# Paired values, maxima in a free row, fp16 triples for K, Q and V, and a loop written out, in a Swin block on one Trainium2 core

## The reference

```
y = roll(ln(x, norm1_g, norm1_b), (-3, -3));  yw = windows(y)            # (B*64, 49, 128)
q, k, v = heads(yw @ qkv_w.T + qkv_b)                                    # 16 heads of 8
attn = softmax(q * 8**-0.5 @ k.T + bias(rel_pos_table) + shift_mask)
o = windows_back((attn @ v) @ proj_w.T + proj_b);  x = x + roll(o, (3, 3))
h = gelu(ln(x, norm2_g, norm2_b) @ fc1_w.T + fc1_b) @ fc2_w.T + fc2_b
return x + h
```

## Time and profile before

| | us |
|---|---|
| median of 3 runs | 4402.23 (4398.28 to 4403.39) |
| the profiled execution | 4409.18, span 4407.4 |
| PE busy | 4134.3 (94%) |
| ACT busy | 2889.0 (66%) |
| DVE busy | 2743.0 (62%) |
| POOL busy | 2014.4 (46%) |
| DMA | 443.34 MB, mean 101 GB/s, q1 32.4% of 16 engines |
| mean granted TensorE clock | 0.983 of full speed |

### The profile page before, as it was taken

The page is one execution under the profiler, slowest core; times in us unless marked ns, Lnnn a source line. Parts: engine busy times, 40 slices in busy tenths (PEclk is TensorE's granted clock), DMA queues, the critical chain, the costliest instruction groups (busy, mean ns, idle before and its releaser), DMA issues.

```text
span 4407.4 us, 179808 instructions
## 1 busy us (share of the span) xinstructions
PE 4134.3 (94%) x72586; PEld 3265.2 (74%) x72586; DVE 2743.0 (62%) x6930; ACT 2889.0 (66%) x5120; POOL 2014.4 (46%) x3472
## 2 busy tenths in 40 slices
PE   3999999999999999999999999999999999999998
PEld 2777777777777777777777777777777777777777
DVE  5666665666656656566565656666566566666663
ACT  2666666666666666666666666766666666666665
POOL 4444444444444444444444444444444444444443
PEclk8999999999999999999999999999999999999999
DMA  2333333333333333333333333333333333333332
GB/s 77 102 106 102 98 105 97 105 102 98 105 99 104 109 95 101 98 105 102 99 104 97 105 101 99 105 101 102 94 105 105 99 104 107 104 104 105 106 106 62
DMA packets 626000, 443.34 MB, mean 101 GB/s; under 512 B 158451, under 2 KB 624611, under 8 KB 625059
## 3 DMA queue, kind: packets, MB, share of 16 engines
q1 hardware_dynamic: 624595, 428.82, 32.4%
q0 software_dynamic: 464, 1.81, 0.1%
HBM read 106.07 MB, written 51.46 MB: 36 GB/s over the span
## 4 chain that ended last, share of the span: by engine, by line
PE 82%; ACT 9%; issue 4%; DVE 3%; SPq 1%; DMA 0%; POOL 0%; ACTq 0%; POOLq 0%; DVEq 0%
PE ps L782 18%; PE ps L752 11%; PE ps L766 10%; PE ps L704 10%; PE ps L816 8%; PE ps L739 7%; PE ps L734 7%; PE ps L850 5%; PE ps L796 3%; DVE neg_max L576 2%; ACT L411 2%; ACT v_own L491 2%; PE ps L809 2%; ACT hid L435 2%; ACT probs L418 2%
## 5 line engine op out<-in xcount | busy, mean ns | idle before, releaser
L576 DVE TENSOR_REDUCE neg_max<-ps 113x16 f32<-113x784 f32 x1024 | 998.1, 975 | 514.5 <-PE ps L704 489.4
L418 ACT ACTIVATE probs<-ps 113x784 f32<-113x784 f32 x1024 | 841.1, 822 | 476.1 <-PE ps L739 470.5
L782 PEld LDWEIGHTS ps<-w,hid 128*112 128x112 f32 x7168 | 845.2, 181 | 49.7 <-issue 18.9
L782 PE MATMUL ps<-w,hid 128*112 128x128 f32 x7168 | 865.9, 277 | 0.0
L435 ACT ACTIVATE hid<-ps,col 128x448 f32<-128x448 f32 (+1 forms) x1024 | 541.6, 585 | 420.9 <-PE ps L766 417.8
L739 PE MATMUL ps<-st_q,st_k 128*49 128x196 f16 x8192 | 701.3, 250 | 4.2 <-issue 4.2
L734 PE MATMUL ps<-bias,eye_k 108*64 108x392 f16 x4096 | 686.6, 332 | 0.0
L752 PE MATMUL ps<-probs,v_own 113*32 113x49 f32 x32768 | 584.8, 211 | 101.0 <-issue 71.2
L752 PEld LDWEIGHTS ps<-probs,v_own 113*32 113x32 f32 x32768 | 438.4, 110 | 275.9 <-issue 245.7
L704 PE MATMUL ps<-mx_k,mx_q 128*49 128x196 f16 x8192 | 547.3, 254 | 20.6 <-DMA mx_k<-k_hi 9.3
L739 PEld LDWEIGHTS ps<-st_q,st_k 128*49 128x49 f16 x8192 | 447.0, 105 | 129.2 <-issue 7.1
(11 more groups left out here) (81 smaller groups left out, 6471.9 us busy)
## 6 DMA issues: line engine op xcount, KB each, us to landing
st_k<-k_hi SPq DMA_DIRECT2D x256, 196.0 KB
st_q<-q_hi SPq DMA_DIRECT2D x1024, 49.0 KB
oT_raw<-pv_sb SPq DMA_DIRECT2D x256, 196.0 KB, 2.6
x_in<-in_x SPq DMA_DIRECT2D x224, 196.0 KB
x_res<-in_x SPq DMA_DIRECT2D x224, 196.0 KB
out_y<-y_out SPq DMA_DIRECT2D x224, 196.0 KB
mx_q<-q_hi SPq DMA_DIRECT2D x128, 196.0 KB
mx_k<-k_hi SPq DMA_DIRECT2D x512, 49.0 KB
```

The source lines that it names most:

```text
L418: nc.scalar.activation(probs[0:KP, w % 2, :].rearrange("p (b c) -> p b c", b=2), ps[0:KP, b:b + 2, 0:HB * WT], ACT.Exp).then_inc(s_exp, 1)
L576: nc.vector.tensor_reduce(neg_max[0:KP, :, w, :], ps[0:KP, 0:2, 0:HB * WT].rearrange("p b (h k) -> p b h k", k=WT), AX_X, ALU.max, negate= ...
L782: last = mm(tokens_of(6)[0:TP, i, :], hid[:, c, i * TP:(i + 1) * TP], w_2[:, c, :], start=(c == 0), stop=(c == CH - 1))
```

## The change

- The hardware loop is gone: `turns` writes all 133 turns out, and every semaphore wait has a constant. The extra semaphore increments of `apart` are gone too.
- The norm's scale and shift (norm1) go into the weights and biases at set-up. ACT writes `yT` as a plain copy (now in the memory of `oT`). DVE splits it into fp16 `yT_hi` and `yT_lo` (new, L599 and L601). K, Q and V each become three fp16 matmuls where there was one in fp32; V takes both images of a window in one stationary operand of 128 columns.
- The negated maxima go by DMA to row 32e + 3 of `st_q`, whose partner rows in `st_k` are set to 1. So `bias` no longer depends on the window, and keeps one copy. The layouts of q, k, `neg_max` and the maxima's PSUM follow.
- Values are multiplied for two pairs of windows (u) at once; `probs` has four buffers; the copy out of PSUM takes both.
- The order of each body changes: on PE the first part of fc2 comes ahead of the transposes, K and Q come after the second part of fc2, all of fc1 comes before V, and each second logits are cut in two. On DVE the reciprocal comes first, and the second copy of V after `x1`. On ACT all gelus come before V's copies.

The diff, cut to its core:

```diff
-        def turns(eng, body):
-            def plain(a, b):
-                for t in range(a, b):
-                    body(t, lambda n: n >= EDGE, lambda k: (t + k) % 2)
-            plain(-2, LOOP_1[0])
-            with eng.Fori(LOOP_1[0], LOOP_1[1] - UNROLL + 1, UNROLL) as t:
-                for later in range(UNROLL):
-                    body(t + later, lambda n: False, lambda k: (LOOP_1[0] + later + k) % 2)
-            plain(LOOP_1[1], STEPS + 3)
+        def turns(body):
+            for t in range(-2, STEPS + 3):
+                body(t, lambda n: n >= EDGE, lambda k: (t + k) % 2)
...
@@ SP: the maxima
-                    for par in range(2):
-                        for im in range(2):
-                            row = MAX_ROWS + im
-                            sp.dma_start(bias[row:row + 1, par, :, :].rearrange("p w c -> p (w c)"),
-                                         neg_maxT[HP * par:HP * (par + 1), im, :]).then_inc(s_neg_dma, 16)
+                    for e in range(EQ):
+                        row = 32 * e + MAX_ROW
+                        sp.dma_start(st_q[odd(0)][row:row + 1, e, :, :].rearrange("p g c -> p (g c)"),
+                                     neg_maxT[32 * e:32 * (e + 1), :, :]).then_inc(s_neg_dma, 16)
...
@@ ACT
-                        return nc.scalar.activation(o, a, ACT.Identity, scale=col[:, G1:G1 + 1],
-                                                    bias=col[:, B1:B1 + 1])
+                        return nc.scalar.activation(o, a, ACT.Copy)
...
@@ DVE: new, ahead of h_lo and behind the reciprocal
+                    high, low = (y[odd(1)][:, :, :, 0:WT].rearrange("p w m q -> p m w q") for y in (yT_hi, yT_lo))
+                    flat = yT[:, :, :, :]
+                    nc.vector.tensor_copy(high, flat).then_inc(s_y_hi, 1)
+                    dve.wait_ge(s_y_hi, n + 1)
+                    nc.vector.tensor_tensor(low, flat, high, ALU.subtract).then_inc(s_y_lo, 1)
...
@@ PE: K and Q
-                    pe.wait_ge(s_yT, n + 1)
-                    for wt, bank in ((w_k, 0), (w_q, 4)):
-                        for im in range(2):
-                            mm(ps[:, bank + im, 0:BT], wt[:, :], yT[odd(1)][:, im, :, :].rearrange("p w q -> p (w q)"),
-                               start=True, stop=True).then_inc(s_qk, 1)
+                    pe.wait_ge(s_y_hi, n + 1)
+                    high, low = ([y[odd(1)][:, :, im, 0:WT] for im in range(2)] for y in (yT_hi, yT_lo))
+                    for w_hi, w_lo, bank in ((wk_hi, wk_lo, 0), (wq_hi, wq_lo, 4)):
+                        for im in range(2):
+                            mm(ps[:, bank + im, 0:BT], w_hi[:, :], high[im], start=True, stop=False)
+                            mm(ps[:, bank + im, 0:BT], w_lo[:, :], high[im], start=False, stop=False)
+                        if bank == 0:
+                            pe.wait_ge(s_y_lo, n + 1)
+                        for im in range(2):
+                            mm(ps[:, bank + im, 0:BT], w_hi[:, :], low[im], start=False, stop=True).then_inc(s_qk, 1)
...
@@ PE: V
-                            for im in range(2):
-                                last = mm(ps[HP * im:HP * im + WT, 6 + b, (w % 4) * C:(w % 4 + 1) * C],
-                                          yT[odd(0)][:, im, w, :], w_v[:, :], start=True, stop=True)
+                            for part, (yy, ww) in enumerate(((yT_hi, wv_hi), (yT_lo, wv_hi), (yT_hi, wv_lo))):
+                                last = mm(ps[:, 6 + b, (w % 4) * C:(w % 4 + 1) * C],
+                                          yy[odd(0)][:, w, :, :].rearrange("p m q -> p (m q)"), ww[:, :],
+                                          start=(part == 0), stop=(part == 2))
...
@@ PE: the attention loop
-                for w in range(NW):
-                    if exists(t):
-                        logits(t, w, edge, odd(0))
-                    if exists(t) and w > 0:
-                        pv(t, w - 1)
-                    if exists(t + 1):
-                        max_logits(t + 1, w, edge)
+                for u in range(NU):
+                    if exists(t):
+                        logits(t, 2 * u, edge, odd(0), (0, 1))
+                        logits(t, 2 * u + 1, edge, odd(0), (0,))
+                    if exists(t + 1):
+                        max_logits(t + 1, 2 * u, edge)
+                    if exists(t):
+                        logits(t, 2 * u + 1, edge, odd(0), (1,))
+                        if u > 0:
+                            pv(t, u - 1)
+                    if exists(t + 1):
+                        max_logits(t + 1, 2 * u + 1, edge)
```

More of the change, by code:

```diff
@@ L43 @@
 BT = NW * WT
+NU = NW // 2
 TP = 2 * W
@@ L182, in exists @@
         def exists(n):
-            return not isinstance(n, int) or 0 <= n < STEPS
+            return 0 <= n < STEPS
         def past(n, k):
-            return not isinstance(n, int) or n > k
+            return n > k
         def loads(n, edge):
@@ L265, in body @@
                 n = t + 2
-                if exists(n) and not (isinstance(n, int) and n == 0):
+                if exists(n) and n != 0:
                     sp.wait_ge(s_t1, n)
@@ L396, in body @@
                     norm(n, s_ln2, mv2, ve2, s_ve2, rs2, s_rs2, mr2, s_mr2, nm2, s_nm2, x1, z2, s_t2, s_z2)
-            turns(pool, body)
+            turns(body)
         @block.scalar
@@ L480, in body @@
                     load_table(ACT.Gelu)
-                    for m in range(6):
+                    for m in range(2 * CH):
                         gelu(t - 2, m)
+                if exists(t):
+                    load_table(ACT.Exp)
                 n = t
@@ L491, in body @@
                         nc.scalar.activation(v_place(1, b), v_made(1, b), ACT.Copy).then_inc(s_vown_b, 1)
[L492 to L494 removed]
                 if exists(t):
[L496 removed]
                     for w in range(NW):
                         exp_pair(t, w)
[L499 to L502 removed]
+                        if w % 2 and w > 1:
+                            copy_pv(t, w // 2 - 1)
+            turns(body)
         @block.vector
@@ L566, in finish @@
                     if past(n, 0):
-                        dve.wait_ge(s_stored, loads(n - 1, edge(n) and (not isinstance(n, int) or edge(n - 1))))
+                        dve.wait_ge(s_stored, loads(n - 1, edge(n) and edge(n - 1)))
                 dve.wait_ge(s_fc2, 2 * n + p + 1)
@@ L668, in body @@
                             aggregate(n, st2, s_st2, mv2, s_ln2)
-            turns(dve, body)
+            turns(body)
         @block.tensor
@@ L680, in _, with group @@
                    start=True, stop=True)
+            pe.wait_ge(s_inita, 2)
+            for c, ww in enumerate((w_q, w_k, w_vp)):
+                last = mm(ps[:, 7, 3 * C + c:3 * C + c + 1], ww, col[:, B1:B1 + 1], start=True, stop=True)
+            last.then_inc(s_w_split, 1)
             pe.wait_ge(s_bv, 1)
-            mm(ps[0:TP, 7, 0:C], bv_wide[:, :], w_p[:, :], start=True, stop=True).then_inc(s_bp_mm, 1)
+            mm(ps[0:TP, 6, 0:C], bv_wide[:, :], w_p[:, :], start=True, stop=True).then_inc(s_bp_mm, 1)
             pe.wait_ge(s_inita, 2)
             pe.wait_ge(s_init, 2)
-            def group(im, bank, g):
-                return ps[HP * im:HP * im + WT, bank + g // 2, (g % 2) * EQ * WT:(g % 2 + 1) * EQ * WT].rearrange(
-                    "p (e q) -> p e q", e=EQ)
+            def group(im, bank, g, step):
+                first = (g % 2) * step
+                return ps[HP * im:HP * im + WT, bank + g // 2, first:first + EQ * WT].rearrange("p (e q) -> p e q", e=EQ)
             def max_logits(n, w, edge):
@@ L730, in logits @@
                 kind = 2 * edge(n) + (w == NW - 1)
                 bank = 2 + 2 * (w % 2)
-                for b in range(2):
+                for b in banks:
                     for im in range(2):
                         mm(ps[HP * im:HP * (im + 1), bank + b, 0:HB * WT], eye_k[0:BIAS_ROWS, kind, im, :],
-                           bias[0:BIAS_ROWS, b, w, :], start=True, stop=False)
+                           bias[0:BIAS_ROWS, b, :], start=True, stop=False)
                     for g in (2 * b, 2 * b + 1):
@@ new lines, in pv @@
+            def pv(n, u):
+                pe.wait_ge(s_exp, NW * n + 2 * u + 2)
+                if u < 2:
+                    pe.wait_ge(s_vown, 2 * n + u + 1)
+                    pe.wait_ge(s_vown_b, 2 * n + u + 1)
+                else:
+                    pe.wait_ge(s_pv_sb, NU * n + u - 1)
+                for w in (2 * u, 2 * u + 1):
+                    for h in range(NH):
+                        g, r = h // NR, h % NR
+                        first = (2 * g + w % 2) * WT
+                        last = mm(ps[32 * r:32 * r + VC, 6 + u % 2, first:first + WT],
+                                  v_own[0:KP, w, h, :], probs[0:KP, w % 4, h * WT:(h + 1) * WT], start=True, stop=True)
@@ L837, in body @@
                 if exists(t - 2):
-                    fc1(t - 2, 4)
```

(3 more changed lines are left out.)

251 lines of the change are left out of this document (125 added, 126 removed).

## The result

The changed kernel takes **4233.77 us** (4232.79 to 4236.54, 4 runs) against 4402.81 for the kernel before in the same session: ratio 0.9619, 95% interval [0.9602, 0.9635]. The direction was forecast, the size was not: −169 us where −34 stood. Its profiled execution took 4236.54 us, span 4234.7.

The account below looks back on a forecast made before the run. It took PE, busy 4134 of 4407 us, plus its losses between matmuls as the bound. From the profiled 4409.2, −144 written out, +105 for turns of 33.28 us, +5 set-up gave 4375, so 4368 us at the median; range 4270 to 4450.

Parts of the forecast that it names:

- part 1: Loop written out: 103 intervals fall to 32.45 us each, −144 us, of which 82 are the 12 returns.
- part 3: End of a turn: PV and first fc2 quarter before L796's transposes remove PE's wait for the last maxima, −0.76 us.
- part 5: Maxima behind the projection: PE waits 1.0 us more before the second maxima matmuls, then 0.1 more three times a turn.
- part 2: Matmuls: fp16 K and Q save 0.67 us a turn, V 0.48; PV of two windows and the maxima's free row nothing.
- part 4: Front of the turn: waits for y_high and y_low add 0.83 us around K, late q_low 0.6 before fc1's later groups.
- set-up: PSUM clear, ten small steps on the weights and four POOL clears before the turns: 0 to 10 us, taken as +5.
- inner losses: Small losses inside a pass of the loop, 0.68 us in each of 91 intervals, 62 us, taken as gone.
- Rival B: Straight code loses in fetching what the loop body lost: 4430 us, or 4455 if all turns lose it; chance 0.14.
- The argument from 20 turns without losses: The last 20 turns, straight code behind the loop, take 32.45 us without the small losses, so written-out turns should too.
- Rival C: V's fp16 matmuls gain nothing and PE does 0.48 us more a turn, 61 us: 4429 us; chance 0.08.
- Rival A: y_high and y_low come in time, so 0.83 and 0.6 us a turn fall away, 183 us: 4185 us; chance 0.08.
- Rival D: The softmax sums land at the late bound, y_high 1.5 us later, +190 us: 4560 us; chance 0.05.

Follow-up runs that it names:

- run 1: The kernel before with its loop written out and nothing else changed, its own matmuls and order kept: 4288.68 us, ratio 0.9734 to the kernel before.
- Run 7: The changed kernel with first maxima matmuls ahead of all second logits and DVE's second copy of V moved to ACT: 4219.07 us.
- run 3: The changed kernel with the values of a pair split again, one window before the logits and one behind: 4317.08 us.
- run 4: The changed kernel with DVE's reciprocal moved behind the cast and the subtraction: 4184.31 us.
- run 11: The changed kernel with reciprocal behind the split, maxima matmuls ahead of logits, V's second copy on ACT, and probabilities and copied V in fp16: 4022.47 us.
- run 2: The changed kernel with K, Q and V back in fp32, without DVE's cast and subtraction: 4294.64 us.

## Why the prediction was wrong

The three runs that undo one part each give the change in its parts, beside what the forecast's own steps gave them:

| part | forecast | measured |
|---|---|---|
| written out (part 1) | −144 | −116 |
| order, pairs, free row (part 3, part 5, the PV of part 2): (−0.76 + 1.0 + 0.3) x 128 | +69 | +6 |
| triples (part 2, 4): (−0.67 − 0.48 + 0.83 + 0.6) x 128 | +36 | −61 |
| set-up | +5 | within the others |
| sum | −34 | −171 |

The measured parts run from the 4404.75 of the kernel before in the session of run 1; they come from three sessions, so each is good to some 5 us. By the prediction's own mark, half a us from 33.3, it is wrong: the mean turn is 32.20.

**Part 1 was right in kind and 28 us too large.** The returns are gone: no interval near 39. The 62 us of inner losses were taken as gone, and they are the step that failed: 22 of them stay in run 1. They had also been counted too wide. These are stretches of the trace of the kernel before, with busy us by engine and, third from the end, the granted clock:

```profile
738.00:748.20 10.20, 6.65 (x60) 6.37 (x61) 0.26 (x1) 2.09 (x5) 0.00 (x0) 0.50 0.31 90
705.13:744.41 39.28, 32.95 (x568) 26.14 (x567) 21.20 (x55) 22.68 (x41) 15.50 (x27) 0.92 0.33 98
744.41:778.93 34.52, 33.70 (x570) 27.11 (x569) 21.20 (x55) 22.45 (x41) 15.49 (x27) 0.94 0.30 90
```

PE stood idle for 4.24 us at the return, and in that time TensorE's granted clock fell from its upper level to its lower one, 1.2 GHz, for 10.2 us; it did so at all 12 returns, during that standstill or less than 1 us behind it, for 6.8 to 10.2 us. There 16 records of fc2 take 3.41 us (744.07 to 747.48), and in straight code 1.74 (4017.58 to 4019.32). So the interval behind a return is long as well. The 12 returns have a mean of 39.32 us and the 12 intervals behind them 34.14: 103 us of the 144 are theirs, and 41 us are left to the other 79. The forecast left out the clock and booked some 20 us of the returns as inner losses. Run 1 has no stretch at the lower level from its set-up to its last turn, and a mean clock of 0.994 against 0.984.

What stays in run 1, 0.18 us a turn, stands at the blocks of instructions. Rival B had that mechanism. The Trainium skill ("Runtime: NRT & Kernel Launch", "Instruction fetch mechanics") calls the cost of crossing from one block to the next mostly hidden; in the dense values it is not. The argument from 20 turns without losses was from one place: run 1 has none in its last 14 turns either, and many before. Why the end of the run is spared stays open.

**Parts 2, 4 and 5 failed, in sizes of terms, all one way, and these decided it.** The forecast said 33.28 us a turn; the turn shown takes 31.79, and from the forecast's terms one comes there:

- K starts at S+6.52. The forecast had PE ready at 6.38 and K from 6.8, behind y_high. Against 6.38 it is +0.14: PE was ready at 6.32 and waited 0.20 us for y_high, where some 0.4 had been forecast.
- K and Q take 2.39 us (4009.77 to 4012.16), 0.41 more than the 1.98 of the sum, where 0.83 stood for the waits ahead of K and in it: −0.42. Of these 2.39 us 2.04 are work and 0.35 the wait for y_low. The sums came when forecast (the reciprocal starts at S+5.27, 5.35 was taken), but the cast took 0.51, not 0.65, the subtraction 0.98, not 1.06, and ACT's pieces, 1.04 for 1.76, ended before either mattered.
- fc1's third group stops for 0.34 (4013.10 to 4013.63, less 0.19), not 0.6: −0.26. ACT's two copies of K took 1.07 and the two of q 1.07 (4011.25 and 4012.20), where 1.25 had been taken for each two.
- V takes 1.35, not 1.40: −0.05. Rival C is dead: the row has 0.056 us for a load and a matmul. By the figure of the Trainium skill ("TensorE: Matmul & The Clock Gate", "Back-to-back issue gap") it would have been 1.94, an estimate; the trace does not agree.
- The second maxima matmuls start at P+2.69 (P = 4022.65), not P+2.95: −0.26. Mechanism, releaser and the length of the wait were right: PE was done with the logits at P+1.73, 0.23 us before the forecast's P+1.96, and waited 0.96 of the 1.0 us. Run 7 takes part of it away.
- A pair of steps takes 3.23, not 1.8 + 1.64 = 3.44: −0.63 for three, the largest of the errors. The step that holds the values takes 1.63 (4026.94 to 4028.57) for 1.8, and 0.13 of that 0.17 is the PV of two windows in one run, which "no gain" in part 2 mis-sized; run 3 shows what such runs are worth, 83 us. The other step is the DVE cycle, 1.60 (4025.34 to 4026.94), where 1.64 was forecast.

33.28 + 0.14 − 0.42 − 0.26 − 0.05 − 0.26 − 0.63 = 31.80. To the mean of 32.20 it is 0.4 a turn, 51 us. The late blocks of instructions account for it: 0.49 us a turn are lost at them, 33 us of which stand as PE's own wait for issue. The forecast did not have them, and by luck they hid part of its error.

Rival A (the front is hidden, 0.08) was nearer in the total, 4185, but not in its mechanism: PE does stop at both places, for 0.55 and 0.34 us, and run 4 shows 50 us of it to be had. Rival D is dead: the sums were there at S+5.27.

## What to carry to other kernels

Where a forecast is a difference of two large terms (here −1.91 of work saved against +2.73 of new waits), tenths taken high in each wait decide the sign: look for each row in the form that the new code will have (a copy without operands is not the activation it replaces), and split by halves of the change before believing the sum. Joining two short runs of small matmuls pays a fixed price once, even where the work is the same. A stop can cost more than its own length: look at the granted clock behind it before sorting losses into kinds. Written-out code takes away the price of a loop's return, but not every loss inside it: count the instructions that an engine goes through per microsecond in its densest stretch.

## What the runs showed of the hardware that was not expected

TensorE's instructions come in blocks of 256, of 64 bytes each. In run 11, with 16,384 records of matmuls (72,080 against 55,696) and as many of loads fewer, q8 moved 2.09 MB less in 128 packets fewer (569 and 9.32 MB against 441 and 7.23). The Trainium skill ("Runtime: NRT & Kernel Launch", "Instruction fetch mechanics") states the same block of 256 instructions; the trace agrees. It adds that fetching hides behind the rate at which instructions are issued, and there the rows speak against it. The fp32 values of two windows are 128 instructions in 0.83 us, the densest stretch of the kernel. There PE stopped for issue, 29.6 us in all; with the values in runs of half the length it was 16.3 us, in run 1, which has them in single windows, 6.0 us, and with half the records nothing at all. All 68 stops stand at one place of a block and end 1.14 to 1.64 us behind the end of a packet; in runs 1, 2 and 3 all 25, 76 and 38 stand and end likewise (the place 192 or 193, 1.19 to 1.67 us).

At a return of the loop PE stood idle for some 4 us, and the granted clock went to its lower level (1.2 GHz) and stayed there for 6.8 to 10.2 us: 16 records of fc2 took 3.41 us for 1.74.

A run of column-tiled fp32 matmuls has a fixed price: 32 records took 0.48 us, 64 took 0.83. ACT wrote 4 x 343 columns from PSUM in 1.04 us as a copy and in 1.76 with scale and shift as operands; DVE took 1.07 us to copy 512 columns of V to fp32 and 1.30 to fp16.
